# Moving a feed-forward loop's input transposition from TensorE to transfers and VectorE, with a new order of its steps and a shorter last unit

## The chip, the cores and the metric

The kernel runs on one core of one Trainium2 chip. The metric is device time in microseconds (us). A run of the kernel before takes 1032.44 us (median of three, 1032.44 to 1032.52).

## What is computed

A layer over 16 batches of 256 tokens with 256 features: attention with 16 heads, then a feed-forward part, each on a normalised input, with its output normalised and added. The change touches only the feed-forward part, which is, in the reference:

```python
wq_gu = ternary_quant(w_gate_up)
gu = jnp.einsum('bsd,hd->bsh', x, wq_gu)
gate, up = jnp.split(gu, 2, axis=-1)
h = jax.nn.silu(gate) * up
hn = rms_norm(h)
wq_p = ternary_quant(w_proj)
return jnp.einsum('bsh,dh->bsd', hn, wq_p)
...
x = x + _layernorm(_L0_attn_ref(_layernorm(x, axis=-1), ...), axis=-1)
x = x + _layernorm(_L0_ffn_ref(_layernorm(x, axis=-1), L0_ffn_w_gate_up, L0_ffn_w_proj), axis=-1)
```

The hidden layer h has 1024 features. The scale of rms_norm is never applied: it goes into the epsilon of the last layer norm, and for that the sum of the squares of h is needed per token.

## The kernel before, in words

The program is written by hand engine by engine. Every engine runs its instructions in the order in which the code lists them, and semaphores join the engines. Attention fills most of the span. The feed-forward part takes the batches as 16 units (u = 0 to 15), one unit per step of a software pipeline. A stage of unit u runs in step u plus the stage's number in the table FLAG; the first seven steps are laced between the last steps of attention. Which instructions an engine issues in one step, and in what order, stands in the function step of that engine.

The path of a unit u, with the lines of the kernel before:

- stats (step u): VectorE takes mean and variance of the 256 features of both token tiles (stats_x2, L1751 and L1754); GpSimd makes scale and bias from them (invert_x2, L673 to L680).
- norm (step u+1): ScalarE writes the normalised rows (norm_x2, L1333, two instructions).
- turn (step u+1): TensorE transposes them in four instructions into a PSUM bank (turn_x2, L1040). ScalarE rounds the bank into a high part (split_x2, L1350) and VectorE makes the low part (split_x2, L1786).
- up (step u+2), in four quarters c = 0 to 3: TensorE multiplies gate and up weights of the quarter (up, L1027, 16 matmuls); ScalarE makes the silu of the gate half (activate, L1310); VectorE multiplies it by the up half (multiply, L1723, called product c below); ScalarE makes the high part (high_hidden, L1317) and the square (square_hidden, L1324) of the product; GpSimd makes the low part (split_hidden, L666); VectorE adds the squares of quarters 1 to 3 onto quarter 0 (add_squares, L1738). Those of quarters 1 and 2 are added in the same step, that of quarter 3 in the next one.
- sum, down, z (step u+3): VectorE folds the two halves of the sum (fold_squares, L1744), TensorE transposes it (sum_tiles, L1049) and VectorE reduces it (sum_floor, L1760 and L1762). TensorE multiplies the hidden parts by the down weights (down, L1067, 32 matmuls); VectorE takes the statistics of the result (stats_z, L1778 and L1781), GpSimd inverts them (invert_z, L687 to L693).
- out (step u+4): ScalarE normalises (norm_z, L1341), GpSimd adds the input (add_x, L701; VectorE for the last unit, L1770) and SP stores.

The gate and up halves alternate between two pairs of PSUM banks, so that quarter c+2 can only be computed once the silu and the product of quarter c are done. The first quarter of a unit waits for the low part of its input (x2_lo_done), the last quarter of down for GpSimd's low part.

Attention already turns its inputs in another way: ScalarE writes the normalised rows in an order of blocks (by_rows, by_blocks), SP moves them between groups of 32 partitions in four transfers (spread_blocks, L489) and VectorE transposes 32 by 32 blocks into PSUM (L1491).

Of the kernel before, what the change touches and what calls it, by code (L numbers as in the profile page):

```python
# [28 lines left out]
P = 128  # L29
# [40 lines left out]
FC = 2  # L70
# [13 lines left out]
def sandwich_kernel(nc, x, wq, wkv, wkvh, wg, wout, wgu, wproj, rope, out):  # L84
    ctx = ExitStack()
    with ctx:
# [44 lines left out]
        def carve(*shape):  # L131
# [157 lines left out]
                                     "turned", "copied"))  # L289
        wgu_placed, wpr_placed = sem("wgu_placed"), sem("wpr_placed")  # L290

        x2_stats, x2_aggr, x2_eps, x2_neg, x2_inv, x2_biased, x2_norm, x2_turned, x2_hi_done, x2_lo_done = (
            sem(f"x2_{k}") for k in ("stats", "aggr", "eps", "neg", "inv", "biased", "norm", "turned", "hi_done",
                                     "lo_done"))
# [3 lines left out]
            sem(k) for k in ("h_added", "h_summed", "sum_ready", "z_squares", "z_floored", "z_ready"))  # L298
        z_stats, z_aggr, z_eps, z_neg, z_inv, z_biased, z_norm, res_done = (
            sem(k) for k in ("z_stats", "z_aggr", "z_eps", "z_neg", "z_inv", "z_biased", "z_norm", "res_done"))  # L300
        tile_done = sem("tile_done")
        stored = [sem(f"stored{i}") for i in range(2)]

# [138 lines left out]
        def _(sp):  # L442
# [97 lines left out]
            over_batches(sp, batch)  # L540

            out_rows = out.rearrange("b (t p) e -> p (b t) e", p=P)
            with sp.Fori(0, BATCH - 3, 2) as u:
                for i in range(2):
                    rows = out_rows[:, bass.ds(address((u + i) * NT), NT), :]
                    sp.wait_ge(res_done, u + i + 1)
                    sp.dma_start(rows, res[i]).then_inc(stored[i], 16)
# [10 lines left out]
        def _(pool):  # L558
# [123 lines left out]
            def invert_z(u, i):  # L682

                pool.wait_ge(z_floored, u + 1)
                pool.wait_ge(z_aggr, u * 2 * NT + 2 * NT)
                at_least(pool, z_norm, u * NT)
                nc.gpsimd.tensor_tensor(z_rstd, z_agg[:, :, 1], z_floor[i], ALU.add).then_inc(z_eps, 1)  # L687
                nc.gpsimd.tensor_tensor(z_minus, z_agg[:, :, 0], minus_one, ALU.mult).then_inc(z_neg, 1)
                pool.wait_ge(z_eps, u + 1)
                nc.gpsimd.tensor_tensor(z_rstd, z_rstd, minus_half[:, 0:NT], ALU.pow).then_inc(z_inv, 1)  # L690
                pool.wait_ge(z_neg, u + 1)
# [21 lines left out]
            def step(u0, s):  # L713
                at = unit_at(u0, s, FLAG["up"])
                if at:
                    split_hidden(*at, 0)
                at = unit_at(u0, s, FLAG["up"])
                if at:
                    split_hidden(*at, 1)
                at = unit_at(u0, s, FLAG["stats"])  # L720
                if at and at[0] > 0:
                    invert_x2(at[0])
                at = unit_at(u0, s, FLAG["z"])
                if at and not last_unit(at[0]):
# [5 lines left out]
                if at and not last_unit(at[0]):  # L730
# [51 lines left out]
        def _(pe):  # L782
# [261 lines left out]
            def sum_tiles(u, i):  # L1044
# [27 lines left out]
            def step(u0, s):  # L1072
                at = unit_at(u0, s, FLAG["up"])
                if at and at[0] > 0:
                    up(*at, 0)
                at = unit_at(u0, s, FLAG["up"])
                if at:
                    up(*at, 1)
                at = unit_at(u0, s, FLAG["down"])
                if at:  # L1080
                    down(*at)
                at = unit_at(u0, s, FLAG["up"])
                if at:
# [5 lines left out]
                if at:  # L1089
                    sum_tiles(*at)  # L1090
                at = unit_at(u0, s, FLAG["up"])
                if at:
                    up(*at, 3)
# [66 lines left out]
        def _(act):  # L1160
# [165 lines left out]
            def norm_x2(u, i, tiles=range(NT)):  # L1326
# [3 lines left out]
                if u == 0:  # L1330
                    act.wait_ge(xt_turned, STEPS)
                for t in tiles:
                    nc.scalar.activation(x2_rows(u, i)[:, t, :], x_batch(u)[:, t, :], ACT.Identity, bias=x2_bias[:, t:t + 1],  # L1333
                                         scale=x2_rstd[:, t:t + 1]).then_inc(x2_norm, 1)

            def norm_z(u, i):
# [15 lines left out]

            def step(u0, s):
                at = unit_at(u0, s, FLAG["out"])
                if at:
                    norm_z(*at)
                at = unit_at(u0, s, FLAG["up"])
                if at:
                    if at[0] > 0:
                        activate(*at, 0)  # L1360
                    high_hidden(*at, 0)
                    activate(*at, 1)
                at = unit_at(u0, s, FLAG["norm"])
                if at and at[0] > 0:
                    norm_x2(*at)
                at = unit_at(u0, s, FLAG["up"])
                if at:
                    high_hidden(*at, 1)
                    square_hidden(*at, 0)
                    square_hidden(*at, 1)  # L1370
# [4 lines left out]
                at = unit_at(u0, s, FLAG["up"])  # L1375
                if at:
                    high_hidden(*at, 2)
                    activate(*at, 3)
                    square_hidden(*at, 2)
# [73 lines left out]
        def _(dve):  # L1453
# [302 lines left out]
            def sum_floor(u, i):  # L1756

                dve.wait_ge(sum_ready, u + 1)
                at_least(dve, z_eps, u - 1)
                nc.vector.tensor_reduce(z_square, heads(O_BANK[:, 0:NT * P], P), AX.X, ALU.add).then_inc(z_squares, 1)  # L1760
# [4 lines left out]
            def add_x(u, i, t):  # L1765

                dve.wait_ge(z_norm, u * NT + t + 1)
                if t == 0:
                    dve.wait_ge(stored[i], (u - i) * 8)
                nc.vector.tensor_tensor(res[i][:, t, :], zn[i][:, t, :], x_batch(u)[:, t, :], ALU.add)\  # L1770
                    .then_inc(tile_done if t < NT - 1 else res_done, 1)

            def stats_z(u, i):
# [16 lines left out]
            def step(u0, s):  # L1790
# [3 lines left out]
                at = unit_at(u0, s, FLAG["out"])  # L1794
                if at and last_unit(at[0]):
                    for t in range(NT):
                        add_x(*at, t)
                at = unit_at(u0, s, FLAG["sum"])
                if at:
                    add_squares(*at, 3)  # L1800
                    if last_unit(at[0]):
                        fold_squares(*at)
                at = unit_at(u0, s, FLAG["up"])
                if at:
                    multiply(*at, 1)
                at = unit_at(u0, s, FLAG["z"])
                if at:
                    stats_z(*at)
                    if not last_unit(at[0]):
                        fold_squares(*at)  # L1810
                at = unit_at(u0, s, FLAG["stats"])
                if at and at[0] > 0:
                    stats_x2(at[0])
                at = unit_at(u0, s, FLAG["up"])
                if at:
                    multiply(*at, 2)
                at = unit_at(u0, s, FLAG["turn"])
                if at and at[0] > 0:
                    split_x2(*at)
                at = unit_at(u0, s, FLAG["z"])  # L1820
                if at:
                    sum_floor(*at)
                at = unit_at(u0, s, FLAG["up"])
# [150 lines left out]
```

## Time and profile before

| | us |
|---|---|
| median of three runs | 1032.44 |
| the profiled execution | 1032.32 |
| its span, first to last instruction | 1030.4 |
| units 2 to 15 of the feed-forward part, from product 1 to product 1 | 854.04 to 1012.14 |

The page gives, for each engine, the busy time in the span. The list of instructions in order of time gives start, duration, line, shapes, and in square brackets how long the engine was idle before it and what ended that idle time. A duration is longer than the distance to the next start of the same engine, since instructions overlap a little; sums below use distances between starts.

### The profile page before, as it was taken

How to read it: one execution, taken by the hardware profiler on the slowest of the kernel's cores; microseconds unless marked ns; L12 is line 12 of the kernel's file. 1: busy time of each engine (PE TensorE's matmuls, PEld its weight loads, DVE VectorE, ACT ScalarE, POOL GpSimd, SP SyncE). 2: the span in 40 equal slices, each digit the busy share in tenths (PEclk: the TensorE clock that was granted, in tenths of full speed). 3: DMA queues.
4: the chain of work that ended last, by engine and by line, in shares of the span. 5: the costliest groups of instructions: out<-in, count | busy, mean ns of one | idle time of the engine just before them, and what ended most of it. 6: DMA issues, size and time to landing. Idle time of an engine off the chain costs nothing. (4 is left out here: it accounts for less than half of the span.)

```text
span 1030.4 us, 25049 instructions
## 1 busy us (share of the span) xinstructions
PE 1013.7 (98%) x7771; PEld 975.1 (95%) x7771; DVE 839.4 (81%) x2871; ACT 862.0 (84%) x2429; POOL 911.0 (88%) x850
## 2 busy tenths in 40 slices
PE   7999999999999999999999999999999999999996
PEld 6899999999999999999999999999999999999996
DVE  6978888888888898889898889887777666676776
ACT  5988888989898989888989898889898867777774
POOL 4888999999999999999999999999899757877775
PEclk9999999999999999999999999999999999999999
DMA  7561121112112211221122122112131000000001
GB/s 255 203 196 48 52 69 52 48 62 69 52 53 60 75 52 48 68 74 55 46 71 71 47 64 67 54 48 73 38 114 32 1 2 12 22 31 22 22 21 42
DMA packets 45587, 64.19 MB, mean 62 GB/s; under 512 B 4512, under 2 KB 26464, under 8 KB 45152
## 3 DMA queue, kind: packets, MB, share of 16 engines
q1 hardware_dynamic: 45456, 62.60, 19.2%
q8 instruction: 62, 1.02, 0.4%
q14 instruction: 69, 0.57, 0.2%
HBM read 50.92 MB, written 9.18 MB: 58 GB/s over the span
## 5 line engine op out<-in xcount | busy, mean ns | idle before, releaser
L649 POOL TENSOR_TENSOR arena<-arena 128x768 f32<-128x768 f32 x128 | 195.9, 1530 | 14.1 <-DVE arena L1618 13.9
L625 POOL TENSOR_TENSOR arena<-arena 128x512 f32<-128x512 f32 x128 | 180.2, 1408 | 10.0
L615 POOL TENSOR_TENSOR arena<-arena,tables 128x512 f32<-128x512 f32 x128 | 165.4, 1292 | 19.9 <-ACT arena L1246 19.3
L1631 DVE SCALAR_TENSOR_TENSOR pt_split<-psum,vh_col,pt_split 128x256 fp32r<-128x256 f32 (+1 forms) x512 | 176.8, 406 | 3.5 <-ACT pt_split L1276 3.0
L638 POOL TENSOR_TENSOR arena<-arena 128x512 f32<-128x512 f32 x127 | 163.3, 1286 | 0.0
L1257 ACT ACTIVATE arena<-arena 128x256 f32<-128x256 f32 x256 | 128.4, 502 | 40.7 <-DVE arena L1608 36.1
L939 PE MATMUL psum<-arena 128*128 128x256 f32 x512 | 153.6, 382 | 3.1 <-POOL arena L625 1.9
L787 PE MATMUL psum<-wo_hi,o_hi 128*128 128x256 f32 x512 | 152.0, 297 | 0.0
L787 PE MATMUL psum<-xt_lo,wq_hi 128*128 128x256 f32 x512 | 144.5, 282 | 0.0
L787 PE MATMUL psum<-xt_hi,wq_lo 128*128 128x256 f32 x512 | 144.4, 282 | 0.0
L787 PE MATMUL psum<-wo_hi,o_lo 128*128 128x256 f32 x512 | 144.2, 282 | 0.0
L787 PE MATMUL psum<-xt_hi,wq_hi 128*128 128x256 f32 x512 | 144.0, 281 | 0.0
L787 PE MATMUL psum<-wo_lo,o_hi 128*128 128x256 f32 x512 | 143.7, 281 | 0.0
L787 PE MATMUL psum<-pt_split,vals_hi 128*128 128x512 f32 (+1 forms) x512 | 142.1, 359 | 0.1
L1027 PE MATMUL psum<-xt_hi,wq_hi 128*128 128x256 f32 x512 | 125.6, 282 | 0.0
L1027 PE MATMUL psum<-xt_lo,wq_hi 128*128 128x256 f32 x512 | 124.4, 284 | 0.0
L1275 ACT ACTIVATE pt_split<-psum,vh_col 128x256 fp32r<-128x256 f32 x256 | 120.6, 471 | 0.5 <-PE psum L958 0.5
L1245 ACT ACTIVATE arena<-psum 64x512 f32<-64x512 f32 x128 | 76.1, 595 | 45.0 <-DVE arena L1593 43.6
L941 PEld LDWEIGHTS psum<-arena 128*128 128x128 f32 x512 | 97.2, 190 | 13.3
L1606 DVE CUSTOM_DVE_ANT_0 arena<-psum,mask 128x256 f32<-128x256 f32 x256 | 106.7, 417 | 0.0
L1640 DVE TENSOR_TENSOR o_lo<-psum,o_hi 128x512 fp32r<-128x512 f32 x128 | 87.1, 681 | 23.6 <-ACT o_hi L1285 22.9
L1259 ACT ACTIVATE arena<-arena 128x128 f32<-128x128 f32 x256 | 99.3, 388 | 0.0
(198 smaller groups left out, 3379.1 us busy)
## 6 DMA issues: line engine op xcount, KB each, us to landing
arena<-kh_rows SPq DMA_DIRECT2D x127, 256.0 KB, 3.4
out<-spare SPq DMA_DIRECT2D x15, 256.0 KB, 2.1
moved<-arena SPq DMA_DIRECT2D x56, 64.0 KB, 2.2
arena<-w_rows SPq DMA_DIRECT2D x6, 512.0 KB, 4.8
X<-L_attn_Wout SPq DMA_DIRECT2D x1, 2048.0 KB, 14.6
X<-L_attn_x SPq DMA_DIRECT2D x1, 2048.0 KB, 10.4
arena<-arena SPq DMA_DIRECT2D x30, 64.0 KB, 2.0
arena<-L_attn_Wq SPq DMA_DIRECT2D x1, 1536.0 KB, 10.5
```

What stands on the lines that cost most here:

```text
L615: nc.gpsimd.tensor_tensor(swap, swap, spread, ALU.mult).then_inc(q_sined, 1)
L625: nc.gpsimd.tensor_tensor(q_rot[p % 2], q_cos[p % 2], q_swap[p % 2], ALU.add).then_inc(q_roped, 1)
L638: nc.gpsimd.tensor_tensor(k_head[p % 2], keys[par].unsqueeze(1).to_broadcast([P, HP, N]), kh_all[p % 4], ALU.mult).then_inc(k_scaled, 1)
L649: nc.gpsimd.tensor_tensor(tb, tb, r.unsqueeze(3).to_broadcast([P, HP, 3, P]), ALU.mult).then_inc(p_ready, 1)
L787: last = nc.tensor.matmul(o, a, b, start=start and i == 0, stop=stop and i == len(passes) - 1, skip_group_check=skip)
L939: nc.tensor.matmul(sj[:, 0:2 * P], q[:, j, P:N], kt[:, j, :], start=True, stop=True, skip_group_check=True)
L1027: last = nc.tensor.matmul(bank[c % 2 * 2 + half][:, j * N:(j + 1) * N], wgu_t[:, k, col:col + P], part[:, k, :], start=n == 0 and j == 0, ...
L1257: nc.scalar.activation(tb[:, j, 0:2 * P], tb[:, j, 0:2 * P], ACT.Exp, scale=-1.0, bias=nmax[p % 4][:, 2 * j:2 * j + 1], accum_out=rsum[p % ...
L1259: nc.scalar.activation(tb[:, j, 2 * P:3 * P], tb[:, j, 2 * P:3 * P], ACT.Exp, scale=-1.0, bias=nmax[p % 4][:, 2 * j + 1:2 * j + 2], accum_ ...
L1275: nc.scalar.activation(pt_hi[p % 2][:, j * N:(j + 1) * N], b[:, 0:N], ACT.Copy, scale=vh[:, 0, h:h + 1])
L1606: nc.vector.tensor_tensor_reduce(tb[:, j, 0:2 * P], S_BANK[j][:, 0:2 * P], mask[:, :], -1.0, -MASKED, ALU.add, ALU.min, nmax[p % 4][:, 2 * ...
L1631: last = nc.vector.scalar_tensor_tensor(pt_lo[p % 2][:, o], b[:, i], vh[:, t, h:h + 1], pt_hi[p % 2][:, o].bitcast(F32), ALU.mult, ALU.sub ...
```

## The change

The transposition of the input of units 1 to 15 leaves TensorE. ScalarE writes the rows in block order, SP issues four transfers per unit, and VectorE transposes into PSUM, as attention does. For this the statistics run one step earlier and so does the norm. Unit 0 stays as it was.

The order in a step changes. On ScalarE the rounding of the input comes before the first square and the norm behind the second one, both ahead of silu 2. On VectorE the transposition, the low part, the fold and the statistics of the next input stand between product 1 and the statistics of the output.

For the last unit the sum of the squares is made by four matmuls against a column of ones, without fold and reduction; VectorE subtracts the mean in PSUM and then scales and adds in one instruction per tile, instead of ScalarE's norm and VectorE's addition. In the last steps GpSimd's order is changed and its additions wait for square sums; square sum 2 comes ahead of the last low part.

```diff
-FLAG = dict(stats=0, norm=1, turn=1, up=2, sum=3, down=3, z=3, out=4)
+FLAG = dict(stats=-1, norm=0, turn=1, up=2, sum=3, down=3, z=3, out=4)
...
+            def move_x2(u):
+
+                sp.wait_ge(x2_norm, u * NT + NT)
+                sp.wait_ge(x2_turned, u)
+                spread_blocks(x2_rows(u, u % 2), x2_moved)
+
+            for u in range(1, 4):
+                move_x2(u)
+            for u in range(BATCH - 2):
+                if u + 4 < BATCH:
+                    move_x2(u + 4)
+                sp.wait_ge(res_done, u + 1)
+                sp.dma_start(out_rows[:, u * NT:(u + 1) * NT, :], res[u % 2]).then_inc(stored[u % 2], 16)
```

GpSimd, waits of add_x, and the order of the last units' step (invert_z also returns ahead of the bias for the last unit):

```diff
                 if isinstance(u, int) and u == BATCH - 2:
-                    pool.wait_ge(h_summed, BATCH)
+                    pool.wait_ge(h_added, BATCH * 3)
+                if isinstance(u, int) and u == BATCH - 3:
+                    pool.wait_ge(h_summed, BATCH - 1)
...
+                at = unit_at(u0, s, FLAG["up"])
+                ending = at and last_unit(at[0])
+                if ending:
+                    add_x(*unit_at(u0, s, FLAG["out"]))
+                    split_hidden(*at, 2)
```

TensorE, the sum for the last unit (in place of sum_tiles) and the transposes that go:

```diff
+            def sum_last(i):
+
+                pe.wait_ge(h_added, BATCH * 3)
+                pe.wait_ge(z_squares, BATCH - 1)
+                for t in range(NT):
+                    for k in range(FC):
+                        last = nc.tensor.matmul(O_BANK[:, t:t + 1], squares[i][:, k, t * P:(t + 1) * P], ones[:, :],
+                                                start=t == 0 and k == 0, stop=k == FC - 1, skip_group_check=True)
+                last.then_inc(sum_ready, 1)
...
-                if at and at[0] > 0:
-                    turn_x2(*at)
```

ScalarE, in norm_x2, and the order of its step:

```diff
+                    o, i_ = x2_rows(u, i)[:, t, :], x_batch(u)[:, t, :]
+                    if u > 0:
+                        o, i_ = by_rows(x2_rows(u, i), t), by_blocks(i_)
...
+                if at:
+                    high_hidden(*at, 1)
+                at = unit_at(u0, s, FLAG["turn"])
+                if at and at[0] > 0:
+                    split_x2(*at)
+                at = unit_at(u0, s, FLAG["up"])
+                if at:
+                    square_hidden(*at, 0)
+                    square_hidden(*at, 1)
                 at = unit_at(u0, s, FLAG["norm"])
                 if at and at[0] > 0:
                     norm_x2(*at)
```

VectorE, the end of the last unit (centre_last, finish_last) and the transposition:

```diff
+            def centre_last(i):
+
+                dve.wait_ge(z_aggr, BATCH * 2 * NT)
+                for t in range(NT):
+                    nc.vector.tensor_scalar(Z_BANK[i][:, t * E:(t + 1) * E], Z_BANK[i][:, t * E:(t + 1) * E],
+                                            z_agg[:, t, 0:1], None, ALU.subtract).then_inc(z_centred, 1)
...
+                nc.vector.scalar_tensor_tensor(res[i][:, t, :], Z_BANK[i][:, t * E:(t + 1) * E], z_rstd[:, t:t + 1],
+                                               x_batch(u)[:, t, :], ALU.mult, ALU.add)\
...
+            def turn_x2(u):
+
+                dve.wait_ge(x2_moved, u * 64)
+                dve.wait_ge(x2_lo_done, u)
+                nc.vector.transpose(turned_out, moved_in).then_inc(x2_turned, 1)
```

VectorE, the order of its step:

```diff
                 if at:
                     multiply(*at, 1)
-                at = unit_at(u0, s, FLAG["z"])
-                if at:
-                    stats_z(*at)
-                    if not last_unit(at[0]):
-                        fold_squares(*at)
+                at = unit_at(u0, s, FLAG["turn"])
+                if at and at[0] > 0:
+                    turn_x2(at[0])
+                    split_x2(*at)
+                at = unit_at(u0, s, FLAG["sum"])
+                if at and not last_unit(at[0]):
+                    fold_squares(*at)
                 at = unit_at(u0, s, FLAG["stats"])
                 if at and at[0] > 0:
                     stats_x2(at[0])
+                at = unit_at(u0, s, FLAG["z"])
+                if at:
+                    stats_z(*at)
                 at = unit_at(u0, s, FLAG["up"])
                 if at:
                     multiply(*at, 2)
-                at = unit_at(u0, s, FLAG["turn"])
-                if at and at[0] > 0:
-                    split_x2(*at)
...
                     add_squares(*at, 1)
                     multiply(*at, 3)
+                    add_squares(*at, 2)
                     if last_unit(at[0]):
                         split_last(*at, 3)
-                    add_squares(*at, 2)
```

## Rows read from the trace of the kernel before

**Rows 1.** The page: the span, then busy us, share and instructions of each engine.

```profile
span 1030.4 us, 25049 instructions
...
PE 1013.7 (98%) x7771; PEld 975.1 (95%) x7771; DVE 839.4 (81%) x2871; ACT 862.0 (84%) x2429; POOL 911.0 (88%) x850
```

**Rows 2.** Chain that ended last, one unit's pieces: start us, us, engine and line.

```profile
973.64 3.83 PE psum L1067 x32
977.48 1.92 PE psum L1027 x16
979.40 0.44 PE psum L1040 x4
```

**Rows 3.** Order of time, VectorE, one unit: start us, us, line, shapes, idle before.

```profile
969.29 0.41 DVE L1760 TENSOR_REDUCE arena<-psum 128x2 f32<-128x256 f32 x1
...
970.42 0.68 DVE L1723 TENSOR_TENSOR arena<-arena,psum 128x512 f32<-128x512 f32 x1
971.02 0.69 DVE L1738 TENSOR_TENSOR arena<-arena 128x512 f32<-128x512 f32 x1
973.72 0.69 DVE L1723 TENSOR_TENSOR arena<-arena,psum 128x512 f32<-128x512 f32 x1 [2.01 <-ACT arena L1310]
974.33 1.73 DVE L1738 TENSOR_TENSOR arena<-arena 128x512 f32<-128x512 f32 x1
975.98 0.68 DVE L1723 TENSOR_TENSOR arena<-arena,psum 128x512 f32<-128x512 f32 x1
977.52 0.76 DVE L1778 BATCH_NORM_STATS2 arena<-psum 128x6 f32<-128x256 f32 x2 [0.86 <-PE psum L1067]
...
978.55 0.42 DVE L1744 TENSOR_TENSOR arena<-arena 128x256 f32<-128x256 f32 x1
...
979.96 0.69 DVE L1723 TENSOR_TENSOR arena<-arena,psum 128x512 f32<-128x512 f32 x1
```

**Rows 4.** Order of time, ScalarE, the same unit.

```profile
971.14 0.63 ACT L1317 ACTIVATE wo_hi<-arena 128x512 fp32r<-128x512 f32 x1 [0.70 <-DVE arena L1723]
971.68 0.61 ACT L1324 ACTIVATE arena<-arena 128x512 f32<-128x512 f32 x1
972.20 1.00 ACT L1341 ACTIVATE arena<-psum,arena 128x256 f32<-128x256 f32 x2
973.10 0.59 ACT L1310 ACTIVATE arena<-psum 128x512 f32<-128x512 f32 x1
...
979.87 0.60 ACT L1350 ACTIVATE xt_hi<-psum 128x512 fp32r<-128x512 f32 x1 [0.80 <-PE psum L1040]
```

**Rows 5.** Order of time, GpSimd, the same unit: low parts of quarters 3 and 0, then 1.

```profile
974.22 3.00 POOL L666 TENSOR_TENSOR wo_lo<-arena,wo_hi 128x512 fp32r<-128x512 f32 x2
977.40 1.28 POOL L666 TENSOR_TENSOR wo_lo<-arena,wo_hi 128x512 fp32r<-128x512 f32 x1 [0.18 <-ACT wo_hi L1317]
```

**Rows 6.** The tile moved in attention: ns min/median/max, first and last start; landing of its transfers.

```profile
L489 SPq DMA_DIRECT2D moved<-arena x56: 597/603/1215, 56.5 to 709.3; - x56
L1491 DVE STREAM_TRANSPOSE psum<-moved x14: 712/722/727, 63.2 to 713.9; 128x512 f32<-128x512 f32 x14
...
DMA to landing us min/median/max: 2.2/2.2/4.1
```

**Rows 7.** Order of time, VectorE: product 1 of unit 2 and of unit 15.

```profile
854.04 0.69 DVE L1723 TENSOR_TENSOR arena<-arena,psum 128x512 f32<-128x512 f32 x1 [0.58 <-ACT arena L1310]
...
1012.14 0.68 DVE L1723 TENSOR_TENSOR arena<-arena,psum 128x512 f32<-128x512 f32 x1
```

**Rows 8.** Order of time, ScalarE: attention's last statistics and norm, in units 2 and 3.

```profile
862.96 0.30 ACT L1189 ACTIVATE arena<-arena,eps 128x2 f32<-128x2 f32 x1 [0.51 <-issue]
...
874.98 1.08 ACT L1197 ACTIVATE arena<-arena 128x256 f32<-128x256 f32 x2
```

**Rows 9.** Chain that ended last: GpSimd's power for the last unit, and the last addition.

```profile
1025.70 0.66 POOL arena L690
...
1027.78 0.42 DVE spare L1770
```

More of the change, by code:

```diff
@@ L290, in sandwich_kernel @@
         wgu_placed, wpr_placed = sem("wgu_placed"), sem("wpr_placed")
+        x2_moved = sem("x2_moved")
         x2_stats, x2_aggr, x2_eps, x2_neg, x2_inv, x2_biased, x2_norm, x2_turned, x2_hi_done, x2_lo_done = (
@@ L300, in sandwich_kernel @@
             sem(k) for k in ("z_stats", "z_aggr", "z_eps", "z_neg", "z_inv", "z_biased", "z_norm", "res_done"))
+        z_centred = sem("z_centred")
         tile_done = sem("tile_done")
@@ L542, in _ @@
             out_rows = out.rearrange("b (t p) e -> p (b t) e", p=P)
[L543 to L547, printed above, removed]
+            def move_x2(u):
[9 more added lines that the diff above has]
+                sp.dma_start(out_rows[:, u * NT:(u + 1) * NT, :], res[u % 2]).then_inc(stored[u % 2], 16)
             sp.wait_ge(res_done, BATCH - 1)
@@ L687, in invert_z @@
                 nc.gpsimd.tensor_tensor(z_rstd, z_agg[:, :, 1], z_floor[i], ALU.add).then_inc(z_eps, 1)
-                nc.gpsimd.tensor_tensor(z_minus, z_agg[:, :, 0], minus_one, ALU.mult).then_inc(z_neg, 1)
+                if not last_unit(u):
+                    nc.gpsimd.tensor_tensor(z_minus, z_agg[:, :, 0], minus_one, ALU.mult).then_inc(z_neg, 1)
                 pool.wait_ge(z_eps, u + 1)
                 nc.gpsimd.tensor_tensor(z_rstd, z_rstd, minus_half[:, 0:NT], ALU.pow).then_inc(z_inv, 1)
+                if last_unit(u):
+                    return
                 pool.wait_ge(z_neg, u + 1)
@@ L726, in step @@
                 at = unit_at(u0, s, FLAG["up"])
-                if at:
+                if at and not ending:
                     split_hidden(*at, 2)
                 at = unit_at(u0, s, FLAG["out"])
-                if at and not last_unit(at[0]):
+                if at and not last_unit(at[0]) and not ending:
                     add_x(*at)
@@ L1085, in step @@
                 at = unit_at(u0, s, FLAG["turn"])
-                if at and at[0] > 0:
-                    turn_x2(*at)
                 at = unit_at(u0, s, FLAG["sum"])
-                if at:
+                if at and not last_unit(at[0]):
                     sum_tiles(*at)
+                if at and last_unit(at[0]):
+                    sum_last(at[1])
                 at = unit_at(u0, s, FLAG["up"])
@@ L1332, in norm_x2 @@
                 for t in tiles:
-                    nc.scalar.activation(x2_rows(u, i)[:, t, :], x_batch(u)[:, t, :], ACT.Identity, bias=x2_bias[:, t:t + 1],
+                    o, i_ = x2_rows(u, i)[:, t, :], x_batch(u)[:, t, :]
+                    if u > 0:
+                        o, i_ = by_rows(x2_rows(u, i), t), by_blocks(i_)
+                    nc.scalar.activation(o, i_, ACT.Identity, bias=x2_bias[:, t:t + 1],
                                          scale=x2_rstd[:, t:t + 1]).then_inc(x2_norm, 1)
@@ L1354, in step @@
                 at = unit_at(u0, s, FLAG["out"])
-                if at:
+                if at and not last_unit(at[0]):
                     norm_z(*at)
@@ L1362, in step @@
                     activate(*at, 1)
+                at = unit_at(u0, s, FLAG["up"])
[4 more added lines that the diff above has]
+                    split_x2(*at)
+                at = unit_at(u0, s, FLAG["up"])
+                if at:
+                    square_hidden(*at, 0)
+                    square_hidden(*at, 1)
                 at = unit_at(u0, s, FLAG["norm"])
@@ L1759, in sum_floor @@
                 at_least(dve, z_eps, u - 1)
+                if last_unit(u):
+                    nc.vector.tensor_scalar(z_floor[i], O_BANK[:, 0:NT], LN_EPS / FF, LN_EPS * RMS_EPS, ALU.mult, ALU.add)\
+                        .then_inc(z_floored, 1)
+                    return
                 nc.vector.tensor_reduce(z_square, heads(O_BANK[:, 0:NT * P], P), AX.X, ALU.add).then_inc(z_squares, 1)
@@ L1763, in sum_floor, with finish_last @@
                     .then_inc(z_floored, 1)
-            def add_x(u, i, t):
-                dve.wait_ge(z_norm, u * NT + t + 1)
+            def centre_last(i):
[3 more added lines that the diff above has]
+                                            z_agg[:, t, 0:1], None, ALU.subtract).then_inc(z_centred, 1)
+            def finish_last(u, i, t):
                 if t == 0:
+                    dve.wait_ge(z_inv, BATCH)
                     dve.wait_ge(stored[i], (u - i) * 8)
-                nc.vector.tensor_tensor(res[i][:, t, :], zn[i][:, t, :], x_batch(u)[:, t, :], ALU.add)\
+                dve.wait_ge(z_centred, t + 1)
+                nc.vector.scalar_tensor_tensor(res[i][:, t, :], Z_BANK[i][:, t * E:(t + 1) * E], z_rstd[:, t:t + 1],
+                                               x_batch(u)[:, t, :], ALU.mult, ALU.add)\
                     .then_inc(tile_done if t < NT - 1 else res_done, 1)
@@ L1796, in step @@
                     for t in range(NT):
-                        add_x(*at, t)
+                        finish_last(*at, t)
                 at = unit_at(u0, s, FLAG["sum"])
@@ L1800, in step @@
                     add_squares(*at, 3)
-                    if last_unit(at[0]):
-                        fold_squares(*at)
                 at = unit_at(u0, s, FLAG["up"])
@@ L1805, in step @@
                     multiply(*at, 1)
+                at = unit_at(u0, s, FLAG["turn"])
[3 more added lines that the diff above has]
+                at = unit_at(u0, s, FLAG["sum"])
+                if at and not last_unit(at[0]):
+                    fold_squares(*at)
+                at = unit_at(u0, s, FLAG["stats"])
+                if at and at[0] > 0:
+                    stats_x2(at[0])
                 at = unit_at(u0, s, FLAG["z"])
@@ L1808, in step @@
                     stats_z(*at)
-                    if not last_unit(at[0]):
[L1810 to L1813, printed above, removed]
                 at = unit_at(u0, s, FLAG["up"])
@@ L1816, in step @@
                     multiply(*at, 2)
-                at = unit_at(u0, s, FLAG["turn"])
-                if at and at[0] > 0:
-                    split_x2(*at)
                 at = unit_at(u0, s, FLAG["z"])
@@ L1822, in step @@
                     sum_floor(*at)
+                    if last_unit(at[0]):
+                        centre_last(at[1])
                 at = unit_at(u0, s, FLAG["up"])
```

5 lines of the change are left out of this document (removed).

## The prediction

> **What bounds the kernel now.** I read the page first: TensorE is busy for 98% of the span, the others for 81 to 88% [rows 1]. That is a mean over two parts, so I read the chain that ended last, in the feed-forward part. It holds nothing but TensorE: a down of 3.83 us, quarters of 1.92 us, four transposes of 0.44 us, each piece beginning where the last ended [rows 2]. With the two transposes of the square sum (half of 0.44, so 0.22) a unit is 4 x 1.92 + 3.83 + 0.44 + 0.22 = 12.17 us. VectorE's own times agree: from product 1 of unit 2 to that of unit 15 are 158.10 us, 12.16 per unit [rows 7]. The reader is then to see in VectorE's order of time where it waits: 0.86 us for the down ahead of the output's statistics, 2.01 us for silu 0 [rows 3]. The first of these waits is the slack that the loop of VectorE and ScalarE has against TensorE: small, 0.86 of 12.17.
>
> **What goes from TensorE.** Units 1 to 15 lose four transposes each, 15 x 0.44 = 6.6 us [rows 2]. If TensorE stayed the bound a unit would take 12.17 - 0.44 = 11.73 us. The question is whether the other engines can do a unit in that.
>
> **What is added, on which path.** VectorE gets a transposition of 0.72 us from SBUF into PSUM [rows 6]. More matters where it stands. In order, a unit's loop through VectorE and ScalarE is now, in distances between starts:
> 1. Product 1 to the transposition, 0.60 (as 970.42 to 971.02 [rows 3]).
> 2. The transposition runs 0.72 [rows 6], then ScalarE rounds, 0.60 [rows 4], then VectorE can begin the low part; two hand-overs between engines of 0.03 each (an estimate: the high part starts 0.72 after the start of a product of 0.68 or 0.69 [rows 3, 4]). Together 1.38. VectorE stands idle for the rounding, since nothing is placed between. Before, TensorE's transposes and that rounding ran beside other work.
> 3. The low part, 0.61 (as large as a product, 973.72 to 974.33), the fold with the input's statistics, 1.41 (978.55 to 979.96; 0.35 and 1.06, an estimate by their durations), the output's, 1.03 [rows 3]. The output's statistics no longer wait for the down.
> Product 1 to product 2: 0.60 + 1.38 + 0.61 + 1.41 + 1.03 = 5.03 us.
> 4. Product 2 to product 3: high part 0.72 later, silu 3 0.54 after it, product 0.62 after that [rows 3, 4], 1.88. VectorE's reduction and square sum 1 take 1.13 from the reduction to the product [rows 3] plus 0.60, 1.73, and lie beside.
> 5. Product 3 to product 0 of the next unit, 3.30, through high part, square, norm of the output and silu, with no idle time on ScalarE between [rows 3, 4].
> 6. Product 0 to product 1, 2.26. Of this square sum 3 took 1.73 us where square sum 2 took 0.69 [rows 3].
> Sum: 5.03 + 1.88 + 3.30 + 2.26 = 12.47 us per unit. That is over 11.73, and over the old 12.17. The same loop before had neither the 1.38 nor the low part ahead of product 2, but 0.86 of waiting; it closed inside TensorE's 12.17. I take TensorE off the bound, with about 0.7 us of idle time per unit.
>
> **Step 6 weighed.** Square sum 3 starts at 974.33, 0.11 us after GpSimd began the low part of quarter 3 at 974.22. GpSimd's two operations take 3.00 us where a lone one takes 1.28 [rows 3, 5]. Both sides lost time, which fits one waiting out the other: 974.22 + 1.28 is 975.5, and 0.5 us later VectorE goes on to product 1. Without the meeting product 1 would follow silu 1, 0.72 + 0.54 + 0.62 = 1.88 after product 0. After the change both chains still start at the reduction: GpSimd's reaches quarter 3 in 974.22 - 969.29 = 4.93 us, VectorE's reaches square sum 3 in 5.04 plus the 0.15 by which product 3 is later (1.28 after the reduction, not 1.13). GpSimd's bias, behind the same square sum 2, gets later too, by 0 to 0.15. At 0, product 1 is tied to GpSimd's end and the loop is 12.32; at 0.15 it is 12.47. I take 12.47, as square sum 2 is moved by just that time.
>
> The Trainium skill ("SBUF — State Buffer", section on SBUF's two separate sides) says that VectorE's instructions with two SBUF inputs and GpSimd's share a port pair as an exclusive lock: whoever starts first has it for its whole instruction. By that rule the order within the 0.11 us decides all, which is rival 2.
>
> **The transfers.** Four issues at 0.60 and a landing of 2.2 us make 1.8 + 2.2 = 4.0 us, up to 5.9 at the longest landing [rows 6]. The norm ends about 4 us behind product 1 and the transposition stands 0.6 behind the next product 1, some 9 us later: hidden. SP's stores wait for GpSimd's addition at the end of a step and the next unit's transfers come later, so neither queues behind the other. If the cover were gone it would cost up to 2 us once, at unit 1, where the pipeline is not yet filled. ScalarE's norm in block order costs what it did: the same shape and engine, cost between 0 and 0.02.
>
> **Sum over the run.** Units 0 and 1 have no output statistics and no outgoing norm yet, so the longer loop is at first filled from slack: walking the same distances from product 1 of unit 0, product 1 of unit 2 comes at 854.05, as before (854.04 [rows 7]). Units 3 and 4 carry attention's last statistics and norm in step 5, 0.9 and 1.0 us on ScalarE, the first with an idle 0.51 [rows 8]. TensorE hid these and now does not. Each takes the place of one meeting of step 6 (-0.4), but the fold then starts behind a low part of quarter 0 or 1 on GpSimd, 0.85 and 0.6 us of waiting (from where those operations would end). Units 3 to 5 take 40.0 us, product 1 of unit 5 comes at 894.0. Eight units at 12.47 give 993.8. The next two have no input statistics: the first also has a norm ahead of silu 2, which then holds product 2, 11.96; the other is 12.47 - 1.06 = 11.4. Product 1 of unit 15 comes at 1017.1, 5.0 later than 1012.14 [rows 7].
>
> The end gives some back. The fold of unit 13 ends 3.0 us after product 1 of unit 14, at 1008.7; TensorE then has 0.22 + 3 x 1.92 + 3.83 + 1.92 + 0.22 + 1.92 = 13.87 us to the last quarter of unit 15 [rows 2], so product 3 is at 1022.6. Then down, 4.0 to the statistics; 1.03 for them and 0.25 for the floor; GpSimd's addition and power, 0.92 with the hand-overs (the power alone is 0.66 [rows 9]), which covers the subtraction of the mean; two last instructions, 0.85; the store, 2.2 (1027.78 + 0.42 to the span's end at 1030.4 [rows 1, 9]). Sum 9.25, span 1031.9. From product 1 of unit 15 this is 14.8 us against 18.3 before: 3.5 given back, by the missing fold, reduction, bias and norm and by no square sum ahead of the statistics. The profiled execution is 1.9 us longer than its span (1032.32 to 1030.4), the median 0.1 longer still: 1033.8 us.
>
> **The rivals.**
> 1. TensorE stays the bound, 11.73 us per unit. Then 6.6 us and the 2.9 of a shorter end go: 1032.4 - 9.5 = 1022.9. For it speaks the old wait of 2.01 us; against it that this wait is behind ScalarE's own unbroken chain of step 5, so it is no slack. Chance 0.12.
> 2. The meeting of step 6 falls away, since GpSimd is 0.1 us later and the square sum gets in first: 12.47 - 0.38 = 12.09 per unit, 4.2 us less over eleven units, 1029.6. For it speaks the thin margin of 0.11; against it that both chains move alike. Chance 0.25.
> 3. Slower: the fold waits behind the low part of quarter 1. That runs from 1.42 to 2.70 us after product 1 (977.40 - 975.98 and 1.28 [rows 3, 5]), the fold is due at 2.59. If GpSimd comes 0.3 us or more later, its whole delay is added, up to one operation, 1.28. At 0.4 per unit it is 4.4 us: 1038. It decides once the low part of quarter 1 begins over 1.5 us behind product 1. Chance 0.2.
> 4. My forecast, 1031 to 1035.5, chance 0.43, the ends from 12.32 and from small further waits.
>
> **How the numbers follow.** The forecast's time is 1033.8. The range reaches from rival 2 with some room to most of rival 3: 1027.5 to 1038. A measurement can tell about 0.2%, 2.1 us, from no change: under 1030.4 is faster, over 1034.5 slower. Faster: rivals 1 and 2, less a little of 2, 0.34. Same: the larger part of the forecast and the rest of rival 2, 0.32. Slower: rival 3 and the upper part of the forecast, 0.34.
>
> **What would show it.** TensorE should have idle time ahead of the sum's transposes (L1049's counterpart), ended by the fold; product 1 to product 1 should be 12.3 to 12.5 us; VectorE should be idle ahead of the low part by 0.65 us, ended by ScalarE's rounding; one square sum per unit should take 1.7 us. A chain of TensorE alone at 11.73 would prove the loop wrongly summed; only short square sums, rival 2; a fold of over 0.8 us, rival 3; a wait for the transfers ahead of the transposition, my cover wrong.

## The result, and the profile after

| | before | after |
|---|---|---|
| median of 19 runs each, us | 1032.44 | 1034.41 |
| profiled execution, us | 1032.32 | 1034.57 |
| its span, us | 1030.4 | 1032.8 |
| product 1 of unit 2 | 854.04 | 854.29 |
| product 1 of unit 15 | 1012.14 | 1016.88 |
| product 1 to product 1, one unit | 12.17 | 12.44 |
| product 3 of unit 15 to the span's end | 12.27 | 10.14 |

The ratio after to before is 1.0021, 95% interval 1.0015 to 1.0027: slower by 1.5 to 2.8 us, just where the forecast drew the line between "same" and "slower" (2.1 us). The time is 0.6 us over the forecast. Some executions of several kernels have the whole feed-forward part 1.2 to 1.4 us later than others (product 1 of unit 2 stands at 854.04 us in the traced execution of the kernel before and at 855.41 in that of a kernel below that is equal up to there), so what follows compares distances, not absolute times.

The page of after, as [rows 1]:

```profile
span 1032.8 us, 24966 instructions
PE 1012.6 (98%) x7717; PEld 970.0 (94%) x7717; DVE 848.8 (82%) x2886; ACT 861.2 (83%) x2427; POOL 914.1 (89%) x848
```

It shows nothing: TensorE is busy for 98% still, although it no longer sets the pace of the feed-forward part. VectorE in order of time, one unit, answering to [rows 3] (start, us, line, shapes, idle time before and what ended it):

```profile
968.64 0.68 DVE L1759 TENSOR_TENSOR arena<-arena,psum 128x512 f32<-128x512 f32 x1
969.24 0.71 DVE L1836 STREAM_TRANSPOSE psum<-moved 128x512 f32<-128x512 f32 x1
970.62 0.69 DVE L1841 TENSOR_TENSOR xt_lo<-psum,xt_hi 128x512 fp32r<-128x512 f32 x1 [0.67 <-ACT xt_hi L1384]
971.23 0.41 DVE L1780 TENSOR_TENSOR arena<-arena 128x256 f32<-128x256 f32 x1
...
973.63 0.69 DVE L1759 TENSOR_TENSOR arena<-arena,psum 128x512 f32<-128x512 f32 x1
...
975.50 0.69 DVE L1759 TENSOR_TENSOR arena<-arena,psum 128x512 f32<-128x512 f32 x1
...
978.81 0.69 DVE L1759 TENSOR_TENSOR arena<-arena,psum 128x512 f32<-128x512 f32 x1 [2.02 <-ACT arena L1341]
979.41 1.75 DVE L1774 TENSOR_TENSOR arena<-arena 128x512 f32<-128x512 f32 x1
981.08 0.68 DVE L1759 TENSOR_TENSOR arena<-arena,psum 128x512 f32<-128x512 f32 x1
```

L1759 is the product, L1836 the transposition, L1841 the low part, L1780 the fold (behind it stand the input's and the output's statistics), L1774 the square sum. See the one place where VectorE stands idle behind its own transposition, 0.67 us, ended by ScalarE's rounding (L1384); no idle time between the fold and product 2, since the output's statistics no longer wait for the down; and the long square sum 3. The same unit's TensorE and GpSimd, in order of time:

```profile
971.70 0.44 PE L1070 MATMUL psum<-ident,arena 128*128 128x128 f32 x2 [0.35 <-DVE arena L1780]
```

```profile
979.29 3.02 POOL L677 TENSOR_TENSOR wo_lo<-arena,wo_hi 128x512 fp32r<-128x512 f32 x2
```

TensorE now waits for the fold ahead of the sum's transposes. Of the 0.7 us per unit in which TensorE starts nothing new (12.44 less 11.73) this row shows half: a matmul is listed with 0.28 us although the next one starts 0.12 later, and so covers the start of a gap. The waits summed over the units (866 to 1012 us: total, times, longest):

```profile
DVE xt_lo L1841 <- ACT xt_hi L1384: 8.0, 12, 0.7
PE psum L1070 <- DVE arena L1780: 5.5, 11, 1.3
```

No row shows a wait for the moved tile: the transfers are hidden. The end, in order of time: GpSimd's power of unit 14, ScalarE's norm of 14 (L1375), GpSimd's addition of 14 (L717), the floor (L1797) and VectorE's last two instructions, which wait for GpSimd's power of unit 15:

```profile
1024.75 1.15 POOL L702 TENSOR_TENSOR arena<-arena,minus_half 128x2 f32<-128x2 f32 x1
...
1026.27 1.02 ACT L1375 ACTIVATE arena<-psum,arena 128x256 f32<-128x256 f32 x2 [1.74 <-POOL arena L707]
...
1027.37 1.26 POOL L717 TENSOR_TENSOR spare<-arena,X 128x512 f32<-128x512 f32 x1 [1.13 <-ACT arena L1375]
1027.47 0.13 DVE L1797 TENSOR_SCALAR arena<-psum 128x2 f32<-128x2 f32 x1
...
1029.60 0.88 DVE L1818 SCALAR_TENSOR_TENSOR spare<-psum,arena,X 128x256 f32<-128x256 f32 x2 [1.12 <-POOL arena L702]
```

The floor is ready at 1027.60, but GpSimd is in the addition of unit 14 until 1028.6; the last instructions start some 0.9 us later than they could.

### The profile page after: what moved, and what is told of

Read it like the earlier page. It is cut to its first block, busy times and chain, and to the rows that moved or that the text cites. A ratio compares the mean times of both kernels' runs of the same rounds, so it can differ in the third digit from the quotient of the medians.

```text
span 1032.8 us, 24966 instructions
## 1 busy us (share of the span) xinstructions
PE 1012.6 (98%) x7717; PEld 970.0 (94%) x7717; DVE 848.8 (82%) x2886; ACT 861.2 (83%) x2427; POOL 914.1 (89%) x848
## 4 chain that ended last, share of the span: by engine, by line
PE 77%; DVE 8%; ACT 5%; issue 5%; POOL 0%; DVEq 0%; ACTq 0%; POOLq 0%
PE psum L808 49%; PE psum L960 10%; PE psum L962 5%; DVE arena L1759 3%; PE psum L978 3%; PE psum L979 3%; PE psum L977 3%; PE psum L1048 2%; ACT arena L1341 2%; DVE arena L1774 1%; ACT arena L1375 1%; PE psum L1098 1%; DVE arena L1787 1%; DVE psum L1836 1%; DVE arena L1827 1%
```

## The experiments

In each, a unit is product 1 to product 1, and the ratio, with its interval, is that to the kernel before, run beside it. The edits are shortened: where an order changes, they show the calls alone.

**What the change's two halves are worth.** The kernel before, with the new end of the last unit alone; it is written as the changed kernel with transfers and order taken back.

```diff
-FLAG = dict(stats=-1, norm=0, turn=1, up=2, sum=3, down=3, z=3, out=4)
+FLAG = dict(stats=0, norm=1, turn=1, up=2, sum=3, down=3, z=3, out=4)
...
-turn_x2(at[0])
```

> The kernel before with only the new end of the last unit (matmuls against ones, mean taken off in PSUM, scaling and addition in one, the reordered last steps of GpSimd and VectorE). Unit time 12.17 as before. From product 3 of the last unit to the span's end before 12.3 us, in the changed kernel 10.1: theory: the run is 2.1 us shorter than before, 1030.3. Rival: the end was shortened by the phase in which the slower loop arrives, and the parts alone give under 1 us.

Measured: 1030.28 us, ratio 0.9977 (0.9968 to 0.9987). The chain that ended last, one unit (start, us, engine and line), as [rows 2]:

```profile
950.70 3.83 PE psum L1094 x32
...
962.87 3.83 PE psum L1094 x32
```

From down to down 12.17 us, TensorE alone, and product 3 of unit 15 to the end 10.08 instead of 12.27. So the end gives 2.2 us and the rest of the change, transfers and order, costs 4.1 us between the medians (1034.41 - 1030.28), or 4.5 by the distance from product 1 of unit 2 to that of unit 15 (162.59 against 158.13). The small net result is a loss with a gain over it.

**Is the idle time for the rounding what the change costs?** The changed kernel, with the input's statistics placed between transposition and low part.

```diff
 turn_x2(at[0])
+stats_x2(at[0])
 split_x2(*at)
 fold_squares(*at)
-stats_x2(at[0])
 stats_z(*at)
```

> The changed kernel, with the statistics of the next input placed on VectorE between the transposition and the low part, where it stands idle for 0.67 us. Theory A (the loop through VectorE and ScalarE sets the unit): product 1 to product 2 falls from 4.99 to about 4.5 us, where ScalarE's chain (rounding, two squares, norm, silu 2) becomes the longer side; the unit goes from 12.44 to about 11.97 us and the run to about 1029. Theory B (the unit is set elsewhere: TensorE with the transfers, or the meeting of square sum 3 with GpSimd alone): the idle time moves and the unit stays at 12.4, the run at 1034.

Measured: 1027.68 us, ratio 0.9958 (0.9941 to 0.9975). VectorE in order of time:

```profile
962.48 0.67 DVE L1759 TENSOR_TENSOR arena<-arena,psum 128x512 f32<-128x512 f32 x1
963.08 0.71 DVE L1836 STREAM_TRANSPOSE psum<-moved 128x512 f32<-128x512 f32 x1
963.71 0.70 DVE L1787 BATCH_NORM_STATS2 arena<-X 128x6 f32<-128x256 f32 x2
...
964.68 0.66 DVE L1841 TENSOR_TENSOR xt_lo<-psum,xt_hi 128x512 fp32r<-128x512 f32 x1
...
966.96 0.69 DVE L1759 TENSOR_TENSOR arena<-arena,psum 128x512 f32<-128x512 f32 x1 [0.27 <-ACT arena L1341]
...
974.41 0.68 DVE L1759 TENSOR_TENSOR arena<-arena,psum 128x512 f32<-128x512 f32 x1
```

No idle time ahead of the low part, a unit is 11.93, and 6.7 us go for one moved call. Theory A holds; the run is 1.3 us under its 1029, mostly since the three units up to product 1 of unit 5 gave 2.4 us (39.38 to 36.97), and not three times the steady 0.51. Product 2 now waits 0.27 us for silu 2: ScalarE's row is the next limit.

**And the norm ahead of silu 2?** The same, with the norm behind silu 2 on ScalarE.

```diff
-norm_x2(*at)
 activate(*at, 2)
+norm_x2(*at)
 high_hidden(*at, 2)
```

> As fill_gap, and ScalarE's norm of the next input behind silu 2, where ScalarE waits for product 2 (1.26 us idle in the changed kernel). Theory A: product 1 to product 2 is 4.3 us, the loop 11.75 us, which is TensorE's own 11.73: TensorE is busy without a gap again, the run at about 1026.5. Theory B: 1034, or as fill_gap.

Measured: 1025.32 us, ratio 0.9933 (0.9916 to 0.9950). The chain that ended last:

```profile
946.47 3.83 PE psum L1098 x32
...
952.43 5.76 PE psum L1048 x48
958.19 1.91 PE psum L1098 x16
```

TensorE alone, 11.72 from down to down: the 0.44 us taken from it are at last worth something. Against the kernel with the new end alone it is 5.0 us (1030.28 - 1025.32), of the 6.6 that the four transposes of 15 units add up to. The same move without the filled gap:

> The changed kernel, with the norm of the next input on ScalarE behind silu 2 instead of ahead of it, and nothing else. With the filled gap the same move was worth 0.3 us per unit. Theory A (here product 2 is held by VectorE's row of transposition, low part, fold and statistics, 4.99 us behind product 1, and silu 2 is done 0.5 us before): 12.44 per unit as in the changed kernel, 1034.4 us within 0.5. Theory B (ScalarE's order is what makes the unit long): 12.1 or less, 1030 us or less.

Measured: 1033.99 us, ratio 1.0015 (1.0005 to 1.0025); a unit (968.49 to 980.94) is 12.45. Theory A: of two limits in a row, the second one is worth nothing while the first stands. The one exception is the unit up to product 1 of unit 14, 11.43 instead of 11.92: without input statistics there, VectorE's row is shorter and the norm ahead of silu 2 was the limit.

**The order of before with the new transposition.** The transposition and low part behind product 2, the output's statistics first, ScalarE as before.

```diff
 multiply(*at, 1)
-turn_x2(at[0]); split_x2(*at)
-fold_squares(*at); stats_x2(at[0]); stats_z(*at)
+stats_z(*at); fold_squares(*at); stats_x2(at[0])
 multiply(*at, 2)
+turn_x2(at[0]); split_x2(*at)
```

> The changed kernel, its transfers and VectorE's transposition kept, but ScalarE and VectorE in the order of the kernel before: transposition and low part behind product 2, the output's statistics ahead of fold and input's statistics, the norm ahead of the high part. Theory A (the path through VectorE and ScalarE is longer by the transposition, 0.72, and the rounding that follows it, 0.66, wherever these stand with nothing between them): product 1 to 2 is 0.60 + 1.03 + 1.41 = 3.04 us, 2 to 3 is 0.60 + 1.38 + 0.61 + 0.53 + 0.61 = 3.73, then 3.31 and 2.27 as measured, 12.35 per unit, 0.09 less than the 12.44 of the changed kernel: about 1033.4 us, and VectorE idle for 0.6 to 0.7 us ahead of the low part, ended by ScalarE's rounding. Theory B (not the transposition but the new order is what costs): 12.17 per unit or less, 1030.3 us or less, since the end is the short one.

Measured: 1045.97 us, ratio 1.0135 (1.0118 to 1.0152). Both theories missed. The chain that ended last, one unit:

```profile
967.86 0.73 DVE psum L1834
...
968.62 0.61 ACT xt_hi L1384
...
969.25 0.70 DVE xt_lo L1839
...
969.99 4.11 PE psum L1048 x32
974.10 3.84 PE psum L1098 x32
...
977.97 0.78 DVE arena L1825 x2
...
979.00 0.53 DVE arena L1778
...
981.14 0.73 DVE psum L1834
```

981.14 - 967.86 = 13.28 us. My sum went round VectorE and ScalarE; this loop goes through TensorE: the low part releases the next unit's first quarters (4.11), these the down (3.84), the down the output's statistics, behind which stand fold, statistics, product 2 and the transposition again. So the new order is no cost: it saves 0.84 us per unit against the old one. The edit moves the transposition with the low part, the output's statistics and ScalarE's order together, so which of these moves the saving needs is not shown. The chain shows what they are up against: from product 1 to the transposition it is 4.59 us here (976.55 to 981.14, with a wait for the down in it), 0.60 in the changed kernel.

**What TensorE's time alone is worth.** The kernel before, with one of four transposes in units 1 to 15.

```diff
-last = nc.tensor.transpose(...)
+if u == 0 or (k == 0 and t == 0):
+    last = nc.tensor.transpose(...)
```

> The kernel before, with one of the four transposes of TensorE for units 1 to 15; three quarters of the transposition are left out, nothing else. It asks what TensorE's time alone is worth. Theory A (before, TensorE is the bound and the path through VectorE and ScalarE has 0.86 us of slack in 12.17): 3 x 0.11 = 0.33 less per unit, 11.84, the chain of waits TensorE alone; 15 x 0.33 = 4.9, some 1027.5 us. Theory B (that path is as long as TensorE's already): product 1 to product 1 stays at 12.1 to 12.17 and the time at 1032 us.

Measured: 1028.99 us, ratio 0.9971 (0.9960 to 0.9982), 3.4 less and not 4.9. From 12.17 the steady unit falls to 11.89, with a chain of TensorE alone (three quarters take 5.82 us, not 5.76, the 0.05 over my 11.84; no row shows why):

```profile
971.13 3.83 PE psum L1068 x32
...
977.21 5.82 PE psum L1027 x48
983.03 3.83 PE psum L1068 x32
```

The early units gained next to nothing: from product 1 of unit 2 to that of unit 5 are 36.38 us, 36.47 in the kernel before. The chain leaves TensorE there between two downs, for the output's statistics and the fold, and these downs are 12.63 us apart:

```profile
863.37 3.85 PE psum L1068 x32
...
868.28 1.30 DVE arena L1745
...
876.00 3.83 PE psum L1068 x32
```

In the kernel before, the chain of the same unit is TensorE alone, and the downs are 12.20 us apart:

```profile
864.12 3.83 PE psum L1067 x32
...
876.32 3.83 PE psum L1067 x32
```

There the fold took 0.85 us and ended at 869.87, 0.44 us ahead of the sum's transposes (870.31). From 851.95 on all downs of the kernel before are 12.16 to 12.20 us apart, with TensorE alone between them. So TensorE was the bound in all these units. The cut takes 0.33 of the 0.44 us of slack, and the fold, which now starts 0.3 us behind one of GpSimd's low parts instead of 0.7, gets 0.45 longer: together more than the slack.

**Is the long square sum 3 a meeting with GpSimd?** GpSimd's low part of quarter 3 made for 16 of 512 columns, once in the changed kernel and once in the kernel before.

```diff
-nc.gpsimd.tensor_tensor(ht_lo[i][:, tiles, :], ...)
+lo, h, hi = (x[i][:, tiles, :] for x in (ht_lo, hid, ht_hi))
+if c == 3:
+    lo, h, hi = (x[:, 0:1, 0:16] for x in (lo, h, hi))
+nc.gpsimd.tensor_tensor(lo, h, hi.bitcast(F32), ALU.subtract)
```

> The changed kernel; GpSimd makes the low part of quarter 3 for 16 of its 512 columns a partition only, so that most of that low part is left out of the result; nothing else differs. Theory A (square sum 3 takes 1.75 us instead of 0.69 because it waits for GpSimd's operation of 1.28 us that began just ahead of it): square sum 3 takes 0.7 to 0.9 us, product 1 follows silu 1 at 1.88 us behind product 0 instead of 2.27, a unit takes 12.05, and 10 units at 0.39 less give 1030.5 us. GpSimd's two operations, 3.02 us together, become 1.3 and some 0.2. Theory B (it is long for another reason, such as its own wait for the square or traffic of the transfers): 1.75 and 12.44 stay, 1034.4 us.

Measured: 1030.87 us, ratio 0.9983 (0.9973 to 0.9992). VectorE in order of time, and GpSimd's shortened operation:

```profile
967.08 0.69 DVE L1761 TENSOR_TENSOR arena<-arena,psum 128x512 f32<-128x512 f32 x1 [0.58 <-ACT arena L1343]
...
977.86 0.69 DVE L1776 TENSOR_TENSOR arena<-arena 128x512 f32<-128x512 f32 x1
979.13 0.69 DVE L1761 TENSOR_TENSOR arena<-arena,psum 128x512 f32<-128x512 f32 x1 [0.58 <-ACT arena L1343]
```

```profile
977.75 0.25 POOL L680 TENSOR_TENSOR wo_lo<-arena,wo_hi 128x16 fp32r<-128x16 f32 x1
```

The square sum is 0.69 instead of 1.75, a unit 12.05 instead of 12.44, to the hundredth what A says. In the kernel before:

> The kernel before with the same edit, for comparison: GpSimd's low part of quarter 3 for 16 of 512 columns, most of it left out of the result. Theory A (there TensorE was the bound and the meeting lay beside it): the square sum gets as short, 0.7 to 0.9 us, but product 1 to product 1 stays at 12.17 us behind unit 5; units 2 to 4, where the fold met GpSimd, may lose up to 1 us in all: 1031.4 to 1032.4 us. Theory B (the meeting held that kernel too): 0.3 us or more per unit less, 1029 us or less.

Measured: 1033.29 us, ratio 1.0009 (1.0000 to 1.0019), 0.9 over A's upper end and far from B. Square sum 3 is 0.69 there too, and from down to down the chain is TensorE alone, 12.16 us:

```profile
950.40 3.83 PE psum L1069 x32
...
962.56 3.83 PE psum L1069 x32
```

The same meeting costs nothing under TensorE and 0.39 us per unit once it no longer covers. The early units, which A let get shorter, got longer: two of them take 12.50 and 12.58 us from down to down instead of 12.20 and 12.16, behind folds of 1.15 and 1.25 us instead of 0.85 and 0.39, each started 0.3 to 0.4 us behind one of GpSimd's low parts.

**Moving the square sum away from the meeting.** The changed kernel, with square sum 3 ahead of product 0.

```diff
+add_squares(*at, 3)
 multiply(*at, 0)
-add_squares(*at, 3)
```

> The changed kernel, with square sum 3 ahead of product 0 on VectorE, in its wait of 2.0 us for silu 0; it then meets no low part of quarter 3 just begun. Theory A with the meeting worth 0.39 us: product 0 to product 1 is 1.88 instead of 2.27, but the square sum now meets another GpSimd operation inside the wait, which pushes GpSimd by about 0.5 us, and the fold may then wait up to 0.4 us behind the low part of quarter 1: unit 12.05 to 12.4 us, run 1030 to 1034. Rival: the order of the two engines doesn't matter since both share what time there is; square sums stay at 1.7 us wherever they stand and the unit at 12.44.

Measured: 1032.92 us, ratio 1.0006 (0.9997 to 1.0016). A unit is 12.20 (967.21 to 979.41):

```profile
976.15 1.24 DVE L1774 TENSOR_TENSOR arena<-arena 128x512 f32<-128x512 f32 x1 [0.62 <-ACT arena L1355]
977.54 0.69 DVE L1759 TENSOR_TENSOR arena<-arena,psum 128x512 f32<-128x512 f32 x1 [0.16 <-ACT arena L1341]
```

Here it starts 0.61 us behind GpSimd's low part of quarter 2 (975.54), takes 1.24 and hides most of it in the wait for silu 0. The fold then meets GpSimd, 0.56 instead of 0.41 (969.81), which explains 12.20 instead of 12.05. A meeting that is moved comes back elsewhere, smaller.

**The end.** The kernel with the filled gap and late norm, with GpSimd's addition of unit 14 behind its power for unit 15, and the stores in that order.

```diff
-add_x(*at)
 invert_z(*at)
+add_x(*at)
```

> The kernel with the filled gap and the late norm (1025.3 us), with GpSimd's addition of unit 14 behind its power for the last unit instead of ahead of it, and a semaphore of its own for the last two tiles. Theory A (that addition, which waits for ScalarE's norm of unit 14, holds the power of the last unit by 0.9 us): product 3 of unit 15 to the end of the span goes from 10.1 to 9.2 to 9.4 us, the time to 1024.5. Theory B (what ends the span is the landing of the stores, or the addition only moves the same work behind): no change, 1025.3.

Measured: 1025.13 us, ratio 0.9930 (0.9913 to 0.9946), 0.2 less than without it, which four executions of each, on different chips, can't tell from nothing. The last instructions, GpSimd, VectorE and SP in order of time:

```profile
1018.98 1.26 POOL L718 TENSOR_TENSOR spare<-arena,X 128x512 f32<-128x512 f32 x1
1019.05 0.88 DVE L1821 SCALAR_TENSOR_TENSOR spare<-psum,arena,X 128x256 f32<-128x256 f32 x2 [0.21 <-POOL arena L703]
...
1020.69 0.47 SPq L564 DMA_DIRECT2D out<-spare  x1
```

The last two instructions start 0.96 us earlier (1019.05 against 1020.01), so A's wait was real. But the store of unit 14 waits for its addition until 1020.2 and is issued at 1020.27, and the last store behind it at 1020.69, only 0.2 earlier than without the edit, where it was the second of these two:

```profile
1020.52 0.82 SPq L563 DMA_DIRECT2D out<-spare  x2
```

From product 3 of unit 15 the span ends no sooner (10.2 us against 10.1). B is right about the time: the addition of unit 14 and its store are the next limit.

## Why the prediction was right, point by point

- *TensorE leaves the bound; the loop of VectorE and ScalarE sets the unit.* Right: 12.44 measured, 12.47 summed. By its steps: product 1 to 2 4.99 (5.03 said), 2 to 3 1.87 (1.88), 3 to 0 3.31 (3.30), 0 to 1 2.27 (2.26). The estimate of 0.03 per hand-over held: the low part starts 1.38 us behind the transposition.
- *The idle time for the rounding.* 0.67 us measured, 0.65 said. It is the cost that decides: filled, it was worth 0.51 per steady unit and 6.7 us in all.
- *The meeting in step 6 stays (12.47, not 12.09).* Right: square sum 3 starts 0.12 behind GpSimd's low part (979.41 and 979.29; 0.11 before) and takes 1.75. GpSimd's bias got longer by 0.13 (0.27 to 0.40), near the 0.15 on which I had settled. Taken away, a unit was 12.05, 0.04 under what rival 2 gave. The Trainium skill ("SBUF — State Buffer", section "SBUF: two separate sides") has an exclusive lock for this pair of instructions. The size agrees: 0.12 behind GpSimd's start, the square sum took 1.75 where waiting out 1.28 would make 1.85, and with the operation cut to 0.25 it took 0.69. The rule that the first one has the lock for its whole instruction does not come out for the short operation: the square sum started at 977.86, inside GpSimd's 977.75 to 978.00, and no wait of 0.14 shows.
- *Rival 3, a fold behind the low part of quarter 1.* Did not come: the fold takes 0.41 in the steady units (0.62 and 0.82 in units 3 and 4, so 0.2 and 0.4 of waiting, where I had 0.85 and 0.6).
- *The walk over the run.* Product 1 of unit 2 at 854.29 (854.05 said), unit 5 893.67 (894.0), unit 13 993.51 (993.8), unit 15 1016.88 (1017.1), product 3 of unit 15 1022.66 (1022.6). That the last one fits to 0.1 is in part luck: the units up to unit 5 took 39.4 and not 40.0, the start was 0.2 late, and one unit took 12.78 for a cause that I had not foreseen (last section), beside 12.44 instead of 12.47 in the others.
- *The transfers are hidden.* Right, no wait for them.
- *The end, 9.25 us.* This term was mis-sized: 10.14. I let the power of unit 15 start with the floor and did not ask what stood ahead of it on GpSimd. The addition of unit 14 did, and it waited for ScalarE's norm of 14, which waited for a power of 1.15 us instead of 0.70, beside VectorE's square sums (that these stretched it is read from the trace alone). From the floor to the last instructions it took 2.13 us where I had 1.17, and this makes the 0.9 us between the span said (1031.9) and the span measured (1032.8); the excess of the time over the span was 0.3 smaller than assumed. The term lacked a second limit too: with that wait taken away the span ended no sooner, since the store of unit 14 then came late. No run takes both away. Of the 3.5 us that the end was to give back, measured from product 1 of unit 15, 2.3 came (18.26 to 15.92).
- *What bounds the kernel before.* Right: from unit 2 on the downs are 12.16 to 12.20 us apart, with TensorE alone between them. But the slack is not the same in every unit: the fold ends 0.87 us ahead of the sum's transposes in the steady units and 0.44 in one early unit. So rival 1, TensorE at 11.73 per unit, was worth less than its 6.6 us even where it came: three of the four transposes brought 3.4 instead of 4.9 us, and the kernel with filled gap and late norm, TensorE's chain again, 5.0.
- *Faster, same or slower.* The forecast lay just inside "within 0.2%"; the 0.9 us of the end moved the time to the border of "slower".

## What to carry to other kernels

Work taken from the engine that is the bound is worth at most the slack of the next loop, which can differ from unit to unit; write that loop out in distances between starts, through every engine, the one that you relieve among them, before and after each reordering. An operation that hands its result to another engine and needs it back should have independent work of its own engine behind it: here one moved call turned a loss of 2 us into a gain of 5, and a second one into 7. A short instruction at the end is late by whatever stands ahead of it in its engine's order, and a store by the store ahead of it.

## What the runs showed of the hardware that was not expected

- An addition of VectorE with both inputs in SBUF and a GpSimd operation of 512 columns on SBUF wait for each other almost whole, in both directions: square sum 3, started 0.12 us behind, takes 1.75 us instead of 0.69, and GpSimd's next low part then 1.77 instead of 1.28 to 1.30. GpSimd's power of 2 columns, started 0.09 us behind a square sum, took 1.15 instead of 0.69. The other way round such short operations did not hold VectorE: square sum 1 starts 0.5 us behind a power in every steady unit, still inside it, and takes 0.68. Products with one input in PSUM (0.65 to 0.69), and the transposition from SBUF to PSUM (0.71 to 0.72 in every unit), kept their durations beside the same operations.
- The aggregations of the output's statistics came 0.35 us late once in each of the seven traces in which these statistics stand behind the low part, always between products 1 and 2 of unit 10 (at 960.98 us in the changed kernel), with 0.46 us of idle time ahead of them. This makes the one unit of 12.78 us. No run here tells why.
